# Linear attention over 64 steps: scores moved ahead of the products with the state, low halves ahead of the states, and a block of scores left out

## The reference

```python
Q = _phi((x @ Wq)...); K = _phi((x @ Wk)...); V = (x @ Wv)...     # _phi(x) = elu(x) + 1
KV = jnp.einsum('bhti,bhtj->bhtij', K, V)
S = jnp.cumsum(KV, axis=2);  z = jnp.cumsum(K, axis=2)
num = jnp.einsum('bhti,bhtij->bhtj', Q, S)
den = jnp.maximum(jnp.einsum('bhti,bhti->bht', Q, z), EPS_DEN)[..., None]
out = (num / den)...reshape(b, t, H * DV) @ Wo
x = x + out;  h = _layernorm(x, ln2_g, ln2_b);  x = x + gelu(h @ Wf1) @ Wf2
```

## Time and profile before

| what | value |
|---|---|
| median of 3 runs | 725.69 us (724.81 to 725.83) |
| span of the profiled execution | 696.0 us |
| median less span | 29.7 us |
| PE busy | 663.0 us, 95% |
| PEld busy | 564.0 us, 81% |
| DVE busy | 530.4 us, 76% |
| ACT busy | 426.3 us, 61% |
| POOL busy | 245.2 us, 35% |
| mean granted TensorE clock | 0.996 |

### The profile page before, as it was taken

The page is one execution under the profiler, slowest core; times in us unless marked ns, Lnnn a source line. Parts: engine busy times, 40 slices in busy tenths (PEclk is TensorE's granted clock), DMA queues, the critical chain, the costliest instruction groups (busy, mean ns, idle before and its releaser), DMA issues.

```text
span 696.0 us, 23152 instructions
## 1 busy us (share of the span) xinstructions
PE 663.0 (95%) x9314; PEld 564.0 (81%) x9314; DVE 530.4 (76%) x1565; ACT 426.3 (61%) x846; POOL 245.2 (35%) x271
## 2 busy tenths in 40 slices
PE   3899999999999999999999999999988999999995
PEld 2678888888888788888888887887778989999983
DVE  4867787887878788877878786898787777666674
ACT  4565576558466845765584668456644655666646
POOL 6200013025313512331253134123315557766664
PEclk9999999999999999999999999999999999999999
DMA  7330010001100100100011001001031224354536
GB/s 251 105 67 17 3 32 17 17 19 48 32 10 13 60 17 15 51 17 17 18 48 32 11 10 32 17 15 36 2 87 47 71 81 131 108 131 148 165 130 185
DMA packets 46521, 40.27 MB, mean 58 GB/s; under 512 B 9104, under 2 KB 41232, under 8 KB 46416
## 3 DMA queue, kind: packets, MB, share of 16 engines
q1 hardware_dynamic: 35360, 25.25, 13.1%
q0 software_dynamic: 4784, 10.39, 4.4%
q10 hardware_dynamic: 6272, 3.16, 1.5%
HBM read 23.12 MB, written 15.66 MB: 56 GB/s over the span
## 4 chain that ended last, share of the span: by engine, by line
PE 78%; DVE 12%; ACT 5%; issue 2%; DMA 1%; POOL 0%; DVEq 0%; ACTq 0%; POOLq 0%
PE banks_o L721 9%; PE banks_sc L563 8%; PE banks_o L542 6%; PE banks_o L554 4%; PE bank_u L535 4%; PE bank_u L569 4%; PE bank_q L434 3%; PE bank_q L436 3%; PE bank_q L435 3%; PE banks_sc L446 3%; PE bank_k L434 2%; PE bank_k L436 2%; PE bank_k L435 2%; DVE work L1257 2%; PE banks_sc L434 2%; PE bank_y L434 2%
## 5 line engine op out<-in xcount | busy, mean ns | idle before, releaser
L1723 POOL DMA_INDIRECT routed_rows<-routed,slot x64 | 63.2, 988 | 148.8 <-PE banks_sc L563 117.1
L827 ACT ACTIVATE work<-bank_u 128x384 f32<-128x384 f32 x64 | 31.5, 492 | 107.5 <-PE bank_u L569 107.5
L1273 DVE TENSOR_TENSOR work<-banks_sc,causal 128x1024 f32<-128x1024 f32 x64 | 77.9, 1218 | 0.6 <-PE banks_sc L563 0.6
L721 PE MATMUL banks_o<-w,work 128*128 x624 | 76.2, 275 | 0.0
L721 PEld LDWEIGHTS banks_o<-w,work 128*128 128x128 f32 x624 | 72.9, 192 | 0.3 <-issue 0.2
L563 PE MATMUL banks_sc<-work 64*64 64x128 f32 x2048 | 70.0, 274 | 1.1 <-ACT v_aug L827 0.7
L542 PE MATMUL banks_o<-v_aug,work 128*64 128x65 f32 x2048 | 70.6, 221 | 0.0
L1257 DVE SCALAR_TENSOR_TENSOR work<-bank_q,work 128x512 f32<-128x512 f32 x64 | 43.8, 684 | 29.4 <-ACT work L892 29.2
L1691 POOL TENSOR_SCALAR ve<-mv 128x4 f32<-128x4 f32 x24 | 4.7, 194 | 174.5 <-DVE mv L1139 174.3
L542 PEld LDWEIGHTS banks_o<-v_aug,work 128*64 128x64 f32 x2048 | 65.3, 138 | 0.0
L1257 DVE SCALAR_TENSOR_TENSOR work<-bank_k,work 128x512 f32<-128x512 f32 x64 | 44.2, 690 | 24.0 <-ACT work L898 24.0
(11 more groups left out here) (324 smaller groups left out, 1796.2 us busy)
## 6 DMA issues: line engine op xcount, KB each, us to landing
work<-in_L_attn_x SPq DMA_DIRECT2D x16, 256.0 KB, 3.4
work<-routed_rows SPq DMA_DIRECT2D x20, 132.0 KB, 2.3
xg_more<-routed_rows SPq DMA_DIRECT2D x19, 132.0 KB, 2.1
stage<-in_L_ffn_w SPq DMA_DIRECT2D x8, 256.0 KB, 2.6
moe_input<-routed SPq DMA_DIRECT2D x8, 256.0 KB, 2.6
work<-moe_input ACTq DMA_DIRECT2D x8, 256.0 KB
v_aug<-expert_results SPq DMA_DIRECT2D x4, 512.0 KB, 6.1
out<-work SPq DMA_DIRECT2D x6, 256.0 KB, 2.9
```

Of the source, the lines that this page charges most:

```text
L721: mm = pe.matmul(Y[t % 2][:, blk(k)], hTe[t % 2][:, f, blk(k)], w2[:, bass.ds(e[t] * F + f * D, D)], start=(f == 0), stop=(f == NF - 1))
L1273: dve.tensor_tensor(am_all, sc_banks.rearrange("p (x s) -> p x s", s=P), causal[:, :].unsqueeze(1).broadcast_to([P, 2 * CH, P]), ALU.mult) ...
L1723: pool.indirect_dma_start(rows_d, bass.IndirectOffsetOnAxis(slot[:, k, c:c + 1], 0), routed[:, c, k, :], None).then_inc(sct, 16)
```

## The change

TensorE: `scores(g)` comes ahead of `across(g-1)`, with a wait for `k_phi` of g in every step; the wait for `v_sb` moves out of `across`. VectorE: `ot_low(g-2)` comes ahead of `states(g-1)`, and `mask(g)` ahead of `normalise(g-1)`. In odd chunks the two halves of 64 tokens change places on the partitions (LOW holds the later tokens). The scores of the later keys of a chunk with its earlier queries, all masked anyway, are not computed: of 16 products of 128 columns, 8 get 64 columns. The masks get a second form for odd chunks, `dest` is corrected for them, and each load or store of a sequence becomes three DMAs, at the start two on SyncE's queue and one on ScalarE's.

```diff
+        def thirds(rows, tile):
+            blocks = rows.rearrange("(c m q) d -> q c m d", m=4, q=DH)
+            return ((tile[:, 0::2, :], rows.rearrange("(c m p) d -> p c m d", m=2, p=P)[:, :, 0, :]),
+                    (tile[LOW, 1::2, :], blocks[:, :, 3, :]), (tile[HIGH, 1::2, :], blocks[:, :, 2, :]))
-        CST_ALL = 14
+        CST_ALL = 16
-            sp.dma_start(xln, x_of(0)).then_inc(ld_xln, 16)
+            load_x(xln, 0, ld_xln, slice(0, 2))
...
+            for to, rows in thirds(x_d[0], xln)[2:]:
+                act.dma_start(to, rows).then_inc(ld_xln, 16)
...
             def across(g):
                 for c in range(1, CH):
-                    if c == 2 and g + 1 < B * PAIRS:
-                        pe.wait_ge(v_sb, min(CH + g + 1, 2 * CH * B))
...
             def scores(g):
-                for c in range(CH):
-                    for n, rows in enumerate(HEADS):
-                        for h, hs in enumerate(HEADS):
-                            mm = pe.matmul((bkE, bkF)[h][rows, blk(c)], kT[cur][hs, blk(2 * c + n, DH)],
-                                           qT[cur][hs, blk(c)], start=True, stop=True)
+                def part(c, n, queries):
+                    at = slice(c * P + queries.start, c * P + queries.stop)
+                    for h, hs in enumerate(HEADS):
+                        mm = pe.matmul((bkE, bkF)[h][HEADS[n], at], kT[g % 2][hs, blk(2 * c + n, DH)],
+                                       qT[g % 2][hs, at], start=True, stop=True)
+                    return mm
+                for c in range(0, CH, 2):
+                    part(c, 0, slice(0, P))
+                    part(c + 1, 1, slice(0, P))
+                    part(c, 1, HIGH)
+                    mm = part(c + 1, 0, LOW)
                 mm.then_inc(sc_mm, 1)
...
-                    across(g - 1)
-
-                if g == 0:
-                    pe.wait_ge(k_phi, 1)
+                pe.wait_ge(k_phi, g + 1)
+                if g > 0:
+                    pe.wait_ge(v_sb, min(CH + g, 2 * CH * B))
                 if g > 1:
                     pe.wait_ge(ot_lo, g - 1)
                 if p == 4 and not first:
                     pe.wait_ge(gelu_sb, b * NF)
                 scores(g)
+                if g > 0:
+                    across(g - 1)
...
-                dve.tensor_tensor(am_all, sc_banks.rearrange("p (x s) -> p x s", s=P),
-                                  causal[:, :].unsqueeze(1).broadcast_to([P, 2 * CH, P]), ALU.mult).then_inc(a_msk, 1)
+                dve.tensor_tensor(am_all.rearrange("p (x m) s -> p x (m s)", m=2),
+                                  sc_banks.rearrange("p (x s) -> p x s", s=2 * P),
+                                  causal[:, :, :].rearrange("p m s -> p (m s)").unsqueeze(1).broadcast_to(
+                                      [P, CH, 2 * P]), ALU.mult).then_inc(a_msk, 1)
...
+                if g > 1 and p != 4:
+                    ot_low(g - 2)
                 if g > 0:
                     states(g - 1)
-                if g > 1 and p != 4:
-                    ot_low(g - 2)
...
+                mask(g)
                 if g > 0:
                     normalise(g - 1)
-                mask(g)
...
+            for rows, by in ((LOW, float(P)), (HIGH, -float(P))):
+                dve.tensor_scalar(dest[rows, 1::2, :], dest[rows, 1::2, :], by, None, ALU.add).then_inc(cst_dve, 1)
+            dve.wait_ge(cst_dve, 3)
```

More of the change, by code:

```diff
@@ L93, in build @@
         ident = sb("ident", [P, P])
-        causal = sb("causal", [P, P])
+        causal = sb("causal", [P, 2, P])
         before = sb("before", [P, P], BF16)
@@ L325, in _, with load_x @@
         def _(sp):
-            sp.dma_start(xln, x_of(0)).then_inc(ld_xln, 16)
+            def load_x(tile, b, done, parts=slice(0, 3)):
+                for to, rows in thirds(x_d[b], tile)[parts]:
+                    sp.dma_start(to, rows).then_inc(done, 16)
+            load_x(xln, 0, ld_xln, slice(0, 2))
             sp.dma_start(w_in[0], wq_d).then_inc(ld_wq, 16)
@@ L334, in load_xln @@
                 sp.wait_ge(f1_mm, b)
-                sp.dma_start(xln, x_of(b)).then_inc(ld_xln, 16)
+                load_x(xln, b, ld_xln)
             def sequence(b):
@@ L351, in store_x3 @@
                 sp.wait_ge(ln_x[2], b + 1)
-                sp.dma_start(x3_d[bass.ds(b * T, T), :].rearrange("(c p) d -> p c d", p=P),
-                             routed[:, :, 0, 0:D]).then_inc(x3_st, 16)
+                for tile, rows in thirds(x3_d[b * T:(b + 1) * T, :], routed[:, :, 0, 0:D]):
+                    sp.dma_start(rows, tile).then_inc(x3_st, 16)
             load_xln(1)
-            sp.dma_start(xres, x_of(0)).then_inc(ld_xres, 16)
+            load_x(xres, 0, ld_xres)
             sp.wait_ge(wof_lo, 3)
@@ L1106, in _ @@
                 if t == EARLY + 1:
-                    act.wait_ge(x3_st, 16 * B)
+                    act.wait_ge(x3_st, 48 * B)
                     act.wait_ge(pad_st, 16 * E)
@@ L1743, in _ @@
             rstds(0, 0)
-            then(pool.memset(causal[:, :], 1.0))
-            then(pool.affine_select(out=causal[:, :], in_=causal[:, :], compare_op=ALU.is_ge, fill=0.0, base=0,
-                                    pattern=[[1, P]], channel_multiplier=-1), False)
+            then(pool.memset(causal[:, :, :], 1.0))
+            then(pool.affine_select(out=causal[:, :, :], in_=causal[:, :, :], compare_op=ALU.is_ge, fill=0.0, base=0,
+                                    pattern=[[0, 2], [1, P]], channel_multiplier=-1))
+            then(pool.affine_select(out=causal[:, 1, LOW], in_=causal[:, 1, LOW], compare_op=ALU.is_ge, fill=1.0,
+                                    base=DH - 1, pattern=[[0, DH]], channel_multiplier=-1), False)
+            then(pool.affine_select(out=causal[:, 1, HIGH], in_=causal[:, 1, HIGH], compare_op=ALU.is_ge, fill=0.0,
+                                    base=-DH, pattern=[[0, DH]], channel_multiplier=1), False)
             then(pool.memset(ones_b[:, :], 1.0))
```

12 lines of the change are left out of this document (5 added, 7 removed).

## The result

The changed kernel took **744.79 us** (743.02 to 751.88, 5 runs) beside 725.46 us (724.81 to 725.83, 5 runs) of the kernel before: ratio **1.028**, 95% interval 1.024 to 1.032. That is 22 us above the forecast of 722.7 and above its range. The profiled run is the one of 751.88 us; its span is 749.8 us.

A forecast was written before the change was run, and what follows sets the result against it. TensorE, 95% busy, bounds the kernel, with VectorE and ScalarE setting its pace as much. Sequences 2 to 6 1.1, 1 -0.16, 7 0.2, 0 2.2, start -0.4: 2.9 us off 725.69 gives 722.7 us; range 716 to 728.

The forecast's parts named there:

- step (0, 1): Second step of sequence 0: scores fill the 1.06 us that `across` waited for the states; gain 0.86 us.
- Paces: TensorE rounds of four products: 0.109 us with 128 columns, 0.058 with 65; scores 0.67 us instead of 0.87.
- Rival B: Slower: narrow rounds cost what wide ones do, mask starts 1.24 us behind scores; 734.6 us, chance 0.16 (B or part).
- (b, 1): Second step of a sequence, counted as a plain step: gain 0.15 us.
- (b, 4): Fifth step of a sequence: scores must wait for the last gelu; loss 0.04 us.
- (b, 0): First step of a sequence, b over 1: `ranks` before it gives the chain time, so no wait; gain 0.53 us.
- (b, 5): Sixth step of a sequence: `residual2` ends later, TensorE arrives 0.5 us earlier and waits at `k_proj`; loss 0.05 us.
- Rival C: No change that can be told: VectorE's chains or the start cost more than summed; 725 us, chance 0.20.
- five places: Places per sequence where VectorE's chains were summed; 0.06 us more in each, over 7 sequences, is 2.1 us.
- plain step: Step without extra parts: TensorE waits for one chain (exps, `ot_high`, `ot_low`) instead of two; gain 0.15 us.
- Steps 2 and 3: Third and fourth steps of a sequence: `stats1` behind `normalise` delays `norm2` and `h2_t`; loss 0.37 us together.
- Sequence 7 as 2 to 6: 0.2: The last sequence was taken to gain 0.2 us, like each of the middle sequences with 0.22.

The follow-up runs named there:

- e0: The kernel before, unchanged, profiled again on a 697 chip: 697.1 us.
- e4: Changed kernel with both orders taken back, keeping narrow scores, exchanged halves and three-part DMAs, on a 725 chip: 718.05 us, ratio 0.989 to the kernel before.
- e3: The changed kernel, unchanged, run again on a 725 chip: 745.65 us, ratio 1.0267 to the kernel before.
- e12: The changed kernel, unchanged, on a 697 chip: 700.96 us, ratio 1.0057 to the kernel before.
- e11: The kernel before, unchanged, on a 697 chip: 696.66 us.
- e5: The kernel before with the new orders alone (full scores, natural row order, one DMA each), on a 725 chip: 752.96 us, ratio 1.038.
- e10: e4 with SyncE's loads held until the sequence's scatters have landed, on a 697 chip: 688.9 us, ratio 0.9875 to the kernel before.
- e17: e4 with every pair of scatters started beside products of 512 columns, on a 725 chip: 709.03 us, ratio 0.979 to the kernel before.
- e15: e10 with the new orders kept in step (0, 1) and in steps (b, 0) of b over 1, on a 725 chip: 716.3 us, ratio 0.989.
- e6: The changed kernel with the old orders in the last four steps of the last sequence, on a 725 chip: 741.11 us.
- e2: The kernel before with three DMAs for each load and store, rows in natural order, on a 697 chip: 697.82 us, ratio 1.0021.
- e14: The changed kernel with SyncE's loads held until the scatters have landed, on a 697 chip: 701.55 us.
- e1: The changed kernel with each sequence load and store as one DMA again, on a 697 chip: 701.12 us, ratio 1.0052 to the kernel before.
- e16: The changed kernel with GpSimd's last two pairs of scatters started in each sequence's second and third steps, on a 725 chip: 732.47 us, ratio 1.009.
- e13: The changed kernel with GpSimd's last two pairs of scatters started in each sequence's second and third steps, on a 697 chip: 701.02 us.

## Why the prediction was wrong

**The base was misread.** The prediction says "The median stands 29.7 us above the span of the profiled execution, which the change doesn't touch". They are a difference between two sorts of chip (e0: 1.7 us between time and span). Both pieces of it lie inside the span: the tail of experts, 175 to 178 us on the 697 chips and 196 to 200 in every trace of a 725 chip, and the steps with scatters. The kernel before left no trace on a 725 chip, so its share is an estimate: 723.2 us of span less 198 of tail leave 525, 6 more than its 518.7 on a 697 chip, which is what six steps (b, 3) of 1 us more would make, close to the 1.1 to 1.7 that e4 shows in the same order. The change does touch that part: it raises the excess of these steps from about 1 us to between 2.7 and 5.8 (e3 beside e12).

**Ledger on one 697 chip** (e11 to e12, us of span, positive is slower):

| stretch | forecast | measured |
|---|---|---|
| start to step (0, 1), step 0 in it | 0.2 | 1.3 |
| (0, 1) to (1, 0) | -2.0 | -1.4 |
| sequence 1 | 0.16 | 0.4 |
| sequences 2 to 6 | -1.1 | 1.0 |
| sequence 7 | -0.2 | 3.3 |
| tail | 0 | 1.2 |
| sum | -2.9 | 5.8 |

The starts of different runs of one kernel differ by about 1 us (22.98 to 24.22 for the kernel before) and the tails by 2, so 1 us in these two lines is no finding. The median of e12 is 3.8 above that of the kernel before beside it. The 3.3 of sequence 7 are 2.0 in steps (7, 4) to (7, 6), 1.4 in (7, 7), 0.5 in (7, 3), less 0.5 gained in the first three.

**Paces, the shorter scores and step (0, 1): right.** 0.69 us to the start of `across` behind a wait, the mask 0.98 behind the scores' start where VectorE is free (forecast 0.96 behind a wait), and step (0, 1) 0.87 us shorter (6.95 to 6.08, forecast 0.86). Rival B (narrow rounds at the wide pace) falls: narrow alone takes 0.18 to 0.20 off six of the eight kinds of step.

**The handover was mis-sized.** The prediction let scores start 0.05 us behind what they wait for, taken from L563 in the earlier trace rows, where the scores had `across` issuing just ahead of them. A group at which TensorE really stands still starts 0.15 behind: `ot_low` ends 194.48, scores 194.63; in step (2, 4) of e12 the last gelu ends at 170.69, scores start at 170.84. That 0.1 us explains (b, 1) and (b, 4). In (b, 0), where nothing is waited for, 0.05 is missing for the fill between scores and `across`, and as much before it; in (b, 5) scores don't wait either, but start 0.05 later and the mask 0.98 behind them instead of 0.91. Four times 0.1 turns the forecast gain of 0.22 a sequence into a loss of 0.18. Rival C, "0.05 to 0.1 us more in the five places than I sum, or the start costs more", came nearest for this part, though it looked for it in VectorE's chains.

**What the two parts are worth was never asked apart.** I set the whole change against before, and read a hidden wait of 0.5 us in a plain step that the orders would shorten. On their own the orders lose 1.7 us (e5, sequence 1), and the narrow scores gain 1.1 a sequence in the old ones (e10, e17). In the old order `across` fills the time in which `ot_low` runs; in the new one TensorE stands there. The gain of (b, 0), 0.43, is real: 0.23 from the order (e15 against e4) and 0.20 from the narrow scores. Steps 2 and 3 came as worked out, -0.31 for -0.37, and `h2_t` waits 0.49 us for `norm2` in e12's rows.

**"Sequence 7 as 2 to 6: 0.2" failed**: -3.3. The register loads of steps (7, 4) to (7, 7) are in the kernel and in its trace, and I counted only instructions with busy time. What had hidden them, the mask, is just what the change moved away: 2.7 us of idle time of VectorE stand behind them in e12, 0.2 in e11. About 1.3 us more are the clock in (7, 7), for which the sum had no term either. e6 shows that both hang on the order: 4.5 us come back with it.

**The DMAs**: the three-part loads cost the kernel before up to 1.3 us (e2), against 0.4 priced for the start and nothing for the rest. ScalarE's issue of the third part takes 0.71 us, not 0.45; its table load comes at 8.76 us in e12 instead of 8.06 (e11), and `q_proj` at 13.63 instead of 12.65. "A whole sequence ahead of use" held: neither held loads (e14, ratio 1.0066) nor one DMA for each (e1, 1.0052) differ from the changed kernel (1.0057) beyond the intervals.

**What the prediction had no term for: scatters beside short products.** On a 725 chip about 15 of the 19 us are this and the clock it costs: 19.3 by the medians, less the 4 of a 697 chip; e16 got 13 of them back. Of the rivals none named it; that the result came out slower, as rival B has it, is no point for B, whose mechanism is not there. Its first explanation in the study, loads beside scatters, was wrong too (e15), and fell only because a kernel with held loads happened to meet a 725 chip.

**What stays open.** Why GpSimd's scatter stops short products, and holds back what TensorE signals, and why on some chips only. That the products' length is what counts, and not something else that goes with it, rests on three places of the scatters (steps (b, 3), (b, 2) and those of e17). The Trainium skill, "DMA: Bandwidth & Descriptors", Terms, says that for DMAs issued by GpSimd the software writes the descriptors to rings in SBUF, where hardware-issued DMAs feed them to the engines directly. No run here shows those rings. A busy way into SBUF and a late stream of instructions are guesses that would both fit, and no run here tells them apart. The tail's extra 20 us bear the same mark: VectorE and ScalarE stand 13 to 19 and 12 to 15 us in waits ended by "remote" there on a 725 chip (three or four and two to four waits), and have none on a 697 chip. That they come from the tail's own 78 indirect stores is likely, but wasn't tried.

## What to carry to other kernels

Before you put a gap between span and median down to overhead, look whether the time and span of one run differ by it; here they didn't, and the gap was work that the trace at hand, from another sort of chip, didn't show. Price an exchange of two instructions by all that was hidden behind each, queue-side register loads too, and price a real stop of TensorE at 0.15 us, not at the 0.05 of a group that follows another. Test a compound change by halves: on a 725 chip one half here gained 1%, the other lost 4%, and GpSimd's indirect DMAs started beside long products rather than short ones gained another 1.1 to 1.3%.

## What the runs showed of the hardware

- Two sorts of chip: 697 and 725 us for the same kernel, within 0.2% on each sort, with a mean granted clock of 0.996 and 0.984. Sequence 1 of the changed kernel, which has no scatters, takes 64.36 us on one (e12) and 64.37 on the other (e3), so these chips are not slower all along.
- On the 725 chips TensorE stops about 0.7 us after a GpSimd indirect DMA that starts beside products of 64 or 65 columns, mostly twice, for 0.3 to 0.5 us each, and consumers start 1.7 to 3.5 us late on its results ("remote"). Where it starts beside products of 512 columns the steps are not longer (10.84 us for (b, 3) in e17, 10.80 for (1, 3), which has no scatter).
- A register load of VectorE with its range test costs its queue 0.6 us (0.30, 0.18 and 0.02 and the gaps between them), hidden as long as the instruction ahead of it lasts.
- Behind a step in which TensorE was busy 7.24 of 9.20 us, its granted clock was 0.59 of full over the next 3.4 us in e12, that is mostly the lower of its levels (1.2 of 2.4 GHz), and full in e13 behind 7.27 of 9.40 us: 6.72 against 5.38 us for the same step, with no difference in the program there (e13 only starts two pairs of scatters earlier in each sequence).
